# Routed expert loops: the turn and the split of the next tile's rows, one weight chunk sooner

## The chip, the core and the metric

The kernel is one program on one core of one Trainium2 chip. Its time is the device time of that core in microseconds (us), from one launch to its end; three runs give a median. Five engines work side by side, each with its own in-order queue: TensorE (PE in the profile, PEld for its weight loads), VectorE (DVE), ScalarE (ACT), GpSimd (POOL) and SyncE (SP, which issues most of the DMAs here). They meet through semaphores only.

## What is computed

Four layers of a gated cross-attention network on 16 sequences of 128 rows of 256 numbers. Each layer adds an attention part and a feed-forward part to x. The feed-forward parts of the first two layers are mixtures of eight experts, of which every row takes two; these are what the change touches. The second one, in the reference:

```python
logits = xt @ router_w.T + routing_bias
probs = jax.nn.sigmoid(logits)
topk_p, topk_idx = jax.lax.top_k(probs, TOP_K)          # TOP_K = 2 of E = 8
...
g = jnp.einsum('th,eih->tei', xt, wg)                    # I = 512
u = jnp.einsum('th,eih->tei', xt, wu)
h = jax.nn.silu(g) * u
y = jnp.einsum('tei,ehi->teh', h, wd)
routed = jnp.einsum('te,teh->th', w, y)
```

The first layer's is of the same form with 1024 in place of 512 and biases b1, b2 and b3; silu is on its first half too.

## The kernel before

**Tiles and chunks.** A router stage sorts the 2 x 2048 (row, expert) pairs by expert into 24 tiles, each of one expert: 15 big ones ("B") of 256 rows and 9 small ones ("S") of 128, in the fixed order BBSBBSBS, three times. `expert_tiles` then runs the same loop for both layers: as `l0m_e` (call in `l0_moe`, from about 297 to 668 us) with NF = 8 chunks of 128 hidden columns, and as `l1m_e` (call in `l1_moe`, from about 938 to 1143 us) with NF = 4. `count(t, f)` = NF t + f numbers the chunks.

**Two-part numbers.** Each fp32 operand is split into a high and a low part, and each product is three matmuls. For a chunk of up weights U, ACT makes the high part UH (line 1645) and DVE the low part UL = U - UH (1720). For the down weights DN, ACT makes DH (1655) and POOL makes DL (1812). For the hidden values ACT makes HH (1676, 1679) and DVE HL (1746, 1749). For the rows of a tile, which PE has turned into columns in PSUM (1561), ACT makes CH (1684) and DVE CL (1755). UH, UL, DH and DL are rings of four chunks; the columns, the weights and the rows have two buffers, by the tile's parity.

**One step (t, f)**, in the order of each queue:

- PE: `up(t, f)` (12 matmuls in a big tile, 6 in a small one; lines 1581, 1588, with a bias matmul at 1594 in l0m_e), `down(t - 1, f)` (6 or 3 matmuls, 1614), for small tiles the turning of their hidden values (1601), and in one step of the tile `turn(t + 1)`, four transposes or two. `up(t, 0)` waits for CH and CL of its tile, every `up` for its UH and UL, every `down` for its DH, DL, HH and HL.
- ACT: UH for the chunk two ahead, DH for two ahead of the down work, HH, silu (1664, 1667), then in one step CH of the next tile, `cols_high(t + 1)`. UH of a tile's first chunk waits for the landing of that tile's up weights. In l1m_e the copy of finished results (1690) stands in front at f = 1.
- DVE: UL for two ahead, the product with silu (1731, 1734, 1738), HL, and in one step CL, `cols_low(t + 1)`. In l0m_e the finished results (1763) stand here at f = 1.
- POOL: DL for each chunk of its tile, after f = 1 the gathers of tile t + 3 (1792, one DMA for each 128 rows), later in the tile the scatters of tile t - 1's results (1801).
- SP: the up weights of tile t when UL of tile t - 2 is done (1444), its down weights when DL of tile t - 2 is done (1455), one after the other.

PE runs down(t - 1) beside up(t), so POOL's DL of a tile is used one tile later than UL of the same tile. The order is written out by hand in the five queues; no planner moves anything. In both loops the step with the turn, CH and CL is f = NF // 2: after chunk 4 of 8, and after chunk 2 of 4.

Of the kernel before, what the change touches and what calls it, by code (L numbers as in the profile page):

```python
# [88 lines left out]
def build(nc, I, out):  # L89
# [20 lines left out]
    with top:  # L110
# [1355 lines left out]
        def expert_tiles(tag, weights, TAB, fill=None, place=None):  # L1466
# [4 lines left out]
            NF = FF // P  # L1471
# [3 lines left out]
            tiles = len(KIND)  # L1475
# [19 lines left out]
            with ExitStack() as c:  # L1495
# [31 lines left out]
                with nc.Block(no_gpsimd_drain=True) as block:  # L1527
# [26 lines left out]
                    def _(pe):  # L1554
# [43 lines left out]
                        def turn_hidden(u):  # L1598
                            pe.wait_ge(s_hr, u + 1)
                            for h in range(2):  # L1600
                                ins = nc.tensor.transpose(pair(hb(u))[:, h, 0:P], HR[:, u % 4, h * P:(h + 1) * P], IDENT)
                            ins.then_inc(s_ht, 1)

                        def down(t, f):
                            n = count(t, f)
                            pe.wait_ge(s_dh, n + 1)
                            pe.wait_ge(s_dl, n + 1)
                            pe.wait_ge(s_hh, at_unit[t, f] + 1)
                            pe.wait_ge(s_hl, at_unit[t, f] + 1)
                            if f == 0 and t >= 2:  # L1610
                                pe.wait_ge(s_ycopy, t - 1)
                            for r in range(R(t)):
                                for p, (h, w) in enumerate(((HH, DH), (HH, DL), (HL, DH))):
                                    ins = nc.tensor.matmul(yb(t)[:, r, :], h[:, t % 2, f, r * P:(r + 1) * P],  # L1614
                                                           w[:, f % RING, :],
                                                           start=(f == 0 and r == 0 and p == 0),
                                                           stop=(f == NF - 1 and r == R(t) - 1 and p == 2),
                                                           skip_group_check=True)
                            ins.then_inc(s_y, 1)
# [5 lines left out]
                        for t in range(tiles + 1):  # L1625
                            for f in range(NF):
                                if t < tiles:
                                    up(t, f)
                                if t >= 1:
                                    down(t - 1, f)  # L1630
                                for u in turn_at.get((t, f), ()):
                                    turn_hidden(u)
                                if f == NF // 2 and t + 1 < tiles:
                                    turn(t + 1)

                    @block.scalar
                    def _(act):
                        def up_high(n):
                            t, f = divmod(n, NF)
                            if t < tiles:  # L1640
                                if f == 0:
                                    act.wait_ge(s_up[t % 2], weights.up_count(t))
                                if n >= RING:
                                    act.wait_ge(s_up_done, n - RING + 1)
                                nc.scalar.copy(UH[:, f % RING, :, :, :],  # L1645
                                               U[:, t % 2, :, :, f * P:(f + 1) * P]).then_inc(s_uh, 1)

                        def down_high(n):
                            t, f = divmod(n, NF)
                            if 0 <= t < tiles:  # L1650
                                if f == 0:
                                    act.wait_ge(s_down[t % 2], 16 * (t // 2 + 1))
                                if n >= RING:
                                    act.wait_ge(s_y, n - RING + 1)
                                nc.scalar.copy(DH[:, f % RING, :], DN[:, t % 2, f, :]).then_inc(s_dh, 1)  # L1655

                        def silu(u):
                            t, f = units[u]
                            if u >= 4:
                                act.wait_ge(s_hr, u - 3)  # L1660
                            if big(t):
                                act.wait_ge(s_up_done, count(t, f) + 1)
                                kw = dict(bias=BU[:, t % 2, 0, f:f + 1]) if bias else {}
                                ins = nc.scalar.activation(SG[:, u % 4, :], hb(u)[:, 0:SLOTS], ACT.Silu, **kw)  # L1664
                            else:
                                act.wait_ge(s_up_done, count(t, f) + 2)
                                ins = nc.scalar.activation(pair(SG[:, u % 4, :]), pair(hb(u))[:, :, 0:P], ACT.Silu)
                            ins.then_inc(s_silu, 1)

                        def hidden_high(u):  # L1670
                            t, f = units[u]
                            if t >= 2:
                                act.wait_ge(s_y, count(t - 2, f) + (1 if big(t) else 2))
                            if big(t):
                                act.wait_ge(s_hr, u + 1)
                                ins = nc.scalar.copy(HH[:, t % 2, f, :], HR[:, u % 4, :])
                            else:
                                act.wait_ge(s_ht, turned(u))
                                ins = nc.scalar.copy(HH[:, t % 2, f:f + 2, 0:P], pair(hb(u))[:, :, 0:P])
                            ins.then_inc(s_hh, 1)  # L1680

                        def cols_high(t):
                            act.wait_ge(s_turn, t + 1)
                            nc.scalar.copy(CH[:, t % 2, :, 0:R(t) * P], cols_v(t)).then_inc(s_ch, 1)

                        def out_rows(t):
                            act.wait_ge(s_y, count(t + 1, 0))
                            if t >= 2:
                                act.wait_ge(s_store[t % 2], rows_upto(t - 2))
                            nc.scalar.copy(Y[:, t % 2, 0:R(t), :], yb(t)).then_inc(s_ycopy, 1)  # L1690

                        if fill is not None:
                            fill.act(act, *fill.EXPERTS)
                        up_high(0)
                        up_high(1)
                        cols_high(0)
                        for t in range(tiles + 1):
                            for f in range(NF):
                                if not bias and f == 1 and t >= 2:
                                    out_rows(t - 2)  # L1700
                                up_high(count(t, f) + 2)
                                down_high(count(t - 1, f) + 2)
                                for u in split_at.get((t, f), ()):
                                    hidden_high(u)
                                if t < tiles and ends(t, f):
                                    silu(at_unit[t, f])
                                if f == NF // 2 and t + 1 < tiles:
                                    cols_high(t + 1)
                        if not bias:
                            out_rows(LAST)  # L1710

                    @block.vector
                    def _(dve):
# [39 lines left out]
                        def cols_low(t):  # L1753
                            dve.wait_ge(s_ch, t + 1)
                            nc.vector.tensor_tensor(CL[:, t % 2, :, 0:R(t) * P], cols_v(t),  # L1755
                                                    CH[:, t % 2, :, 0:R(t) * P].bitcast(F32), ALU.subtract).then_inc(s_cl, 1)
# [14 lines left out]
                        for t in range(tiles + 1):  # L1771
                            for f in range(NF):
                                up_low(count(t, f) + 2)
                                if t < tiles and ends(t, f):
                                    hidden(at_unit[t, f])
                                for u in split_at.get((t, f), ()):
                                    hidden_low(u)
                                if bias and f == 1 and t >= 2:
                                    out_rows(t - 2)
                                if f == NF // 2 and t + 1 < tiles:  # L1780
                                    cols_low(t + 1)
                        if bias:
                            out_rows(LAST)
# [1976 lines left out]
```

## Time and profile before

| | us |
|---|---|
| runs | 1606.39, 1607.42, 1613.87 |
| median | 1607.42 |
| profiled execution, its own time | 1603.92 |
| its span, first to last instruction | 1602.1 |
| PE busy over the span | 1324.1 (83%) |
| DVE busy | 1130.4 (71%) |
| ACT busy | 906.0 (57%) |
| POOL busy | 728.4 (45%) |
| mean granted TensorE clock, of full speed | 0.912 |

A busy time is the sum of an engine's instruction times; a matmul's end is modelled, 0.28 us after its start where the next one starts 0.12 us after it. "Idle before, releaser" is the time an engine stood before an instruction and what ended it; "issue" means that the profile shows nothing it waited for. Start times are from the span's start.

### The profile page before, as it was taken

To read this page: it belongs to the slowest core of one execution; us is meant where nothing else is said; L and a number is where in the kernel's file an instruction comes from. 1 tells how busy PE (TensorE), PEld (TensorE's weight loads), DVE (VectorE), ACT (ScalarE), POOL (GpSimd) and SP (SyncE) were. 2 spreads that over 40 slices of the span, in tenths; PEclk is the share of its full clock that TensorE was granted. 3 is DMA by queue.
4 is the path that set the end of the run, shared out by engine and by line. 5 is a ranking of instruction groups with operands and counts; after the bars stand their busy time and mean duration, and the time that the engine had idled before them with its cause. 6 is when DMAs were issued, how large, how long until landed. Compare 5 with 4: busy or idle time off the path is not lost. (4 is left out here: it accounts for less than half of the span.)

```text
span 1602.1 us, 28284 instructions
## 1 busy us (share of the span) xinstructions
PE 1324.1 (83%) x9624; PEld 1110.0 (69%) x9642; DVE 1130.4 (71%) x2469; ACT 906.0 (57%) x1952; POOL 728.4 (45%) x753
## 2 busy tenths in 40 slices
PE   2689977899999999869974779899778965555898
PEld 0445555799999999735554779899776842345687
DVE  6447756688988988559966558778565649785654
ACT  3236652677877877457732447777426347464432
POOL 2223202367777777413321038888403930454444
PEclk8699997999999999889995789999899979676899
DMA  5000003456656656320014027676511000101000
GB/s 186 1 1 1 1 14 127 180 221 247 269 219 258 262 216 258 109 63 1 1 56 166 4 91 250 225 242 240 184 39 50 1 0 1 33 1 62 1 27 27
DMA packets 60780, 173.69 MB, mean 108 GB/s; under 512 B 10256, under 2 KB 42000, under 8 KB 51040
## 3 DMA queue, kind: packets, MB, share of 16 engines
q1 hardware_dynamic: 53152, 151.42, 26.4%
q0 software_dynamic: 7488, 20.46, 3.7%
q8 instruction: 81, 1.33, 0.4%
q14 instruction: 59, 0.48, 0.1%
HBM read 155.34 MB, written 16.52 MB: 107 GB/s over the span
## 5 line engine op out<-in xcount | busy, mean ns | idle before, releaser
L1812 POOL TENSOR_TENSOR l0m_e_DL<-l0m_e_DN,l0m_e_DH 128x256 fp32r<-128x256 f32 x192 | 183.4, 965 | 86.6 <-ACT l0m_e_DH L1655 85.5
L1720 DVE TENSOR_TENSOR l0m_e_UL<-l0m_e_U,l0m_e_UH 128x512 fp32r<-128x512 f32 x192 | 164.5, 862 | 10.7 <-ACT l0m_e_UH L1645 10.4
L1581 PE MATMUL PS<-l0m_e_CH,l0m_e_UH 128*128 128x256 f32 x480 | 138.5, 289 | 2.0 <-DVE l0m_e_CL L1755 2.0
L1581 PE MATMUL PS<-l0m_e_CH,l0m_e_UL 128*128 128x256 f32 x480 | 136.5, 284 | 0.0
L1581 PE MATMUL PS<-l0m_e_CL,l0m_e_UH 128*128 128x256 f32 x480 | 136.4, 284 | 0.0
L1645 ACT CAST l0m_e_UH<-l0m_e_U 128x512 fp32r<-128x512 f32 x192 | 118.1, 615 | 0.0
L1720 DVE TENSOR_TENSOR l1m_e_UL<-l1m_e_U,l1m_e_UH 128x512 fp32r<-128x512 f32 x96 | 85.5, 892 | 19.9 <-ACT l1m_e_UH L1645 19.2
L1812 POOL TENSOR_TENSOR l1m_e_DL<-l1m_e_DN,l1m_e_DH 128x256 fp32r<-128x256 f32 x96 | 85.2, 899 | 25.5 <-ACT l1m_e_DH L1655 24.4
L1581 PEld LDWEIGHTS PS<-l0m_e_CH,l0m_e_UH 128*128 128x128 f32 x480 | 92.8, 193 | 2.2 <-ACT l0m_e_UH L1645 2.2
L1581 PEld LDWEIGHTS PS<-l0m_e_CL,l0m_e_UH 128*128 128x128 f32 x480 | 92.9, 194 | 0.0
L1581 PEld LDWEIGHTS PS<-l0m_e_CH,l0m_e_UL 128*128 128x128 f32 x480 | 92.7, 193 | 0.0
L1614 PE MATMUL PS<-l0m_e_DH,l0m_e_HH 128*128 128x256 f32 x312 | 89.0, 285 | 4.1 <-issue 3.9
L1614 PE MATMUL PS<-l0m_e_DH,l0m_e_HL 128*128 128x256 f32 x312 | 88.6, 284 | 0.0
L1614 PE MATMUL PS<-l0m_e_DL,l0m_e_HH 128*128 128x256 f32 x312 | 88.6, 284 | 0.0
L1655 ACT CAST l0m_e_DH<-l0m_e_DN 128x256 fp32r<-128x256 f32 x192 | 78.1, 408 | 0.2 <-PE PS L1614 0.2
L1581 PE MATMUL PS<-l1m_e_CH,l1m_e_UH 128*128 128x256 f32 x240 | 71.8, 299 | 7.7 <-DVE l1m_e_CL L1755 6.2
L3505 POOL TENSOR_TENSOR Z<-l3f_WI,Z 128x512 f32<-128x512 f32 x32 | 50.7, 1586 | 58.6 <-DVE Z L3601 53.5
L1734 DVE SCALAR_TENSOR_TENSOR Z<-PS,l0m_e_BU,Z 128x256 f32<-128x256 f32 x120 | 57.4, 478 | 27.7 <-ACT Z L1664 27.3
L525 POOL TENSOR_TENSOR l1a_KBD<-CTX,CONST 128x512 f32<-128x512 f32 x32 | 33.1, 1039 | 92.7 <-PE PS L548 48.2
L525 POOL TENSOR_TENSOR l0a_KBD<-l0a_KT,CONST 128x512 f32<-128x512 f32 x32 | 33.4, 1046 | 91.3 <-PE PS L548 62.6
L1645 ACT CAST l1m_e_UH<-l1m_e_U 128x512 fp32r<-128x512 f32 x96 | 59.7, 623 | 24.6 <-DMA l1m_e_U<-in_l_up 18.5
L1746 DVE TENSOR_TENSOR l0m_e_HL<-Z,l0m_e_HH 128x256 fp32r<-128x256 f32 x120 | 72.5, 604 | 0.0
(610 smaller groups left out, 4752.9 us busy)
## 6 DMA issues: line engine op xcount, KB each, us to landing
l0m_e_U<-in_l_up SPq DMA_DIRECT2D x24, 2048.0 KB
l0m_e_DN<-in_l_down SPq DMA_DIRECT2D x24, 1024.0 KB, 5.0
l1m_e_U<-in_l_up SPq DMA_DIRECT2D x24, 1024.0 KB, 6.4
l1m_e_DN<-in_l_down SPq DMA_DIRECT2D x24, 512.0 KB, 3.9
CTX<-in_ctx SPq DMA_DIRECT2D x2, 2048.0 KB, 10.4
l1a_GA<-results_by_choice SPq DMA_DIRECT2D x16, 256.0 KB, 6.0
l1m_c_GA<-results_by_choice SPq DMA_DIRECT2D x16, 256.0 KB, 4.7
Z<-in_l_b_rows SPq DMA_DIRECT2D x24, 128.0 KB
```

What stands on the lines that cost most here:

```text
L525: nc.gpsimd.tensor_tensor(KBD[:, h % KR, :, :], KT[:, chunk, b * S:(b + 1) * S].rearrange("p (o s) -> p o s", o=1) .broadcast_to([P, 4, S] ...
L1581: ins = nc.tensor.matmul(hb(u)[:, a * SLOTS:(a + 1) * SLOTS], w[:, f % RING, k, a, :], x[:, t % 2, k, :], start=(p == 0), stop=(p == len(p ...
L1614: ins = nc.tensor.matmul(yb(t)[:, r, :], h[:, t % 2, f, r * P:(r + 1) * P], w[:, f % RING, :], start=(f == 0 and r == 0 and p == 0), stop= ...
L1645: nc.scalar.copy(UH[:, f % RING, :, :, :], U[:, t % 2, :, :, f * P:(f + 1) * P]).then_inc(s_uh, 1)
L1655: nc.scalar.copy(DH[:, f % RING, :], DN[:, t % 2, f, :]).then_inc(s_dh, 1)
L1720: nc.vector.tensor_tensor(UL[:, f % RING, :, :, :], U[:, t % 2, :, :, f * P:(f + 1) * P], UH[:, f % RING, :, :, :].bitcast(F32), ALU.subtr ...
L1734: ins = nc.vector.scalar_tensor_tensor(out=HR[:, u % 4, :], in0=hb(u)[:, SLOTS:2 * SLOTS], scalar=BU[:, t % 2, 1, f:f + 1], in1=SG[:, u % ...
L1746: ins = nc.vector.tensor_tensor(HL[:, t % 2, f, :], HR[:, u % 4, :], HH[:, t % 2, f, :].bitcast(F32), ALU.subtract)
L1812: nc.gpsimd.tensor_tensor(DL[:, f % RING, :], DN[:, t % 2, f, :], DH[:, f % RING, :].bitcast(F32), ALU.subtract).then_inc(s_dl, 1)
L3505: nc.gpsimd.tensor_tensor(HR(u), HA(u), HB(u), ALU.add).then_inc(s_h, 1)
```

## The change

In each of the three compute queues the step in which the next tile's rows are turned (PE), made into CH (ACT) and into CL (DVE) is one earlier: f = NF // 2 - 1, which is 3 instead of 4 in l0m_e and 1 instead of 2 in l1m_e. The place within the step stays the last. Nothing else is touched, no instruction is added or taken out, and each wait stays with its instruction.

```diff
@@ @block.tensor
                                 for u in turn_at.get((t, f), ()):
                                     turn_hidden(u)
-                                if f == NF // 2 and t + 1 < tiles:
+                                if f == NF // 2 - 1 and t + 1 < tiles:
                                     turn(t + 1)
@@ @block.scalar
                                 if t < tiles and ends(t, f):
                                     silu(at_unit[t, f])
-                                if f == NF // 2 and t + 1 < tiles:
+                                if f == NF // 2 - 1 and t + 1 < tiles:
                                     cols_high(t + 1)
@@ @block.vector
                                 if bias and f == 1 and t >= 2:
                                     out_rows(t - 2)
-                                if f == NF // 2 and t + 1 < tiles:
+                                if f == NF // 2 - 1 and t + 1 < tiles:
                                     cols_low(t + 1)
```

## Rows read from the trace of the kernel before

**Rows 1.** Windows, a stretch inside each loop: busy us (instructions), clock, DMA share, GB/s

```profile
core 0: us, PE busy (x) PEld busy (x) DVE busy (x) ACT busy (x) POOL busy (x), PEclk, DMA share, GB/s
320.00:650.00 330.00, 328.78 (x2758) 328.35 (x2758) 290.92 (x502) 260.39 (x655) 241.60 (x242) 1.00 0.63 240
960.00:1128.00 168.00, 157.64 (x1283) 153.64 (x1282) 135.37 (x230) 127.64 (x333) 141.69 (x146) 1.00 0.69 240
```

**Rows 2.** Waits, 320 to 650 us: who <- whom: total us, times, longest

```profile
DVE l0m_e_CL L1755 <- ACT l0m_e_CH L1684: 10.8, 8, 1.7
...
PE PS L1614 <- issue: 1.2, 2, 0.6
```

**Rows 3.** Waits, 900 to 1160 us, around L1's loop

```profile
ACT l1m_e_UH L1645 <- DMA l1m_e_U<-in_l_up: 18.5, 15, 2.5
...
ACT l1m_e_CH L1684 <- PE PS L1561: 13.5, 13, 4.8
...
PE PS L1581 <- DVE l1m_e_CL L1755: 6.2, 7, 1.5
...
PE PS L1561 <- DMA l1m_e_ROW<-rows_by_token,l1m_TOKEN: 5.6, 1, 5.6
...
PE PS L1588 <- DVE l1m_e_CL L1755: 2.3, 2, 1.6
...
PE PS L1581 <- issue: 1.5, 7, 0.3
```

**Rows 4.** Timeline, tile 8 to 9 of L1: start, us, engine, what, [idle before]

```profile
1012.47 0.62 ACT L1645 CAST l1m_e_UH<-l1m_e_U 128x512 fp32r<-128x512 f32 x1 [2.14 <-DMA l1m_e_U<-in_l_up]
...
1013.19 0.69 DVE L1720 TENSOR_TENSOR l1m_e_UL<-l1m_e_U,l1m_e_UH 128x512 fp32r<-128x512 f32 x1 [1.74 <-ACT l1m_e_UH L1645]
...
1013.81 0.28 PE L1614 MATMUL PS<-l1m_e_DH,l1m_e_HL 128*128 128x256 f32 x1
1013.88 0.58 ACT L1684 CAST l1m_e_CH<-PS 128x512 fp32r<-128x512 f32 x1
...
1014.35 0.63 ACT L1645 CAST l1m_e_UH<-l1m_e_U 128x512 fp32r<-128x512 f32 x1
...
1014.69 0.68 DVE L1755 TENSOR_TENSOR l1m_e_CL<-PS,l1m_e_CH 128x512 fp32r<-128x512 f32 x1
...
1015.63 0.36 PE L1581 MATMUL PS<-l1m_e_CH,l1m_e_UH 128*128 128x256 f32 x1 [1.54 <-DVE l1m_e_CL L1755]
```

**Rows 5.** Waits of POOL, 960 to 1128 us

```profile
POOL l1m_e_DL L1812 <- ACT l1m_e_DH L1655: 11.7, 17, 1.1
```

**Rows 6.** Timeline of POOL in L1's loop: three second DLs of a tile

```profile
981.36 0.74 POOL L1812 TENSOR_TENSOR l1m_e_DL<-l1m_e_DN,l1m_e_DH 128x256 fp32r<-128x256 f32 x1 [0.40 <-ACT l1m_e_DH L1655]
...
1015.36 1.22 POOL L1812 TENSOR_TENSOR l1m_e_DL<-l1m_e_DN,l1m_e_DH 128x256 fp32r<-128x256 f32 x1 [0.88 <-ACT l1m_e_DH L1655]
...
1116.20 0.94 POOL L1812 TENSOR_TENSOR l1m_e_DL<-l1m_e_DN,l1m_e_DH 128x256 fp32r<-128x256 f32 x1 [1.04 <-ACT l1m_e_DH L1655]
```

**Rows 7.** Timeline of PE in L1's loop: first tile, a down step, an "issue" boundary

```profile
940.56 0.55 PE L1581 MATMUL PS<-l1m_e_CH,l1m_e_UH 128*128 128x256 f32 x1 [1.49 <-DVE l1m_e_CL L1755]
...
1002.81 0.35 PE L1614 MATMUL PS<-l1m_e_DH,l1m_e_HH 128*128 128x256 f32 x1 [1.22 <-issue]
...
1006.02 0.35 PE L1581 MATMUL PS<-l1m_e_CH,l1m_e_UH 128*128 128x256 f32 x1 [0.17 <-issue]
```

**Rows 8.** Timeline of DVE and PE in L0's loop, tile 8, chunks 4 to 6

```profile
427.75 1.22 DVE L1720 TENSOR_TENSOR l0m_e_UL<-l0m_e_U,l0m_e_UH 128x512 fp32r<-128x512 f32 x1
...
429.79 0.68 DVE L1755 TENSOR_TENSOR l0m_e_CL<-PS,l0m_e_CH 128x512 fp32r<-128x512 f32 x1
...
430.13 0.28 PE L1581 MATMUL PS<-l0m_e_CH,l0m_e_UH 128*128 128x256 f32 x1
...
430.38 0.93 DVE L1720 TENSOR_TENSOR l0m_e_UL<-l0m_e_U,l0m_e_UH 128x512 fp32r<-128x512 f32 x1
```

**Rows 9.** The page's costliest groups: busy us, mean ns | idle before, releaser

```profile
L1812 POOL TENSOR_TENSOR l0m_e_DL<-l0m_e_DN,l0m_e_DH 128x256 fp32r<-128x256 f32 x192 | 183.4, 965 | 86.6 <-ACT l0m_e_DH L1655 85.5
...
L1812 POOL TENSOR_TENSOR l1m_e_DL<-l1m_e_DN,l1m_e_DH 128x256 fp32r<-128x256 f32 x96 | 85.2, 899 | 25.5 <-ACT l1m_e_DH L1655 24.4
```

## The prediction, made before the changed kernel had run

> **What bounds the kernel now.** The page makes TensorE (PE) the busiest engine, at 83% of the span, but a share is an average, so I asked for stretches. The diff touches only the two routed loops, L0's (8 weight chunks a tile) and L1's (4 chunks a tile). In L0's loop PE is busy for 328.78 of 330 us, at a granted clock of 1.00, which is the 2.4 GHz level; in L1's it is 157.64 of 168, at the same clock [rows 1]. So the change can win only in L1, about 10 us at most, and can lose in L0. The waits say what the gaps are. In L0 PE waited 1.2 us in all, never for the split columns CL [rows 2]. In L1 it waited for CL 6.2 + 2.3 us in nine places, and seven waits of 1.5 us in all stand as "issue" [rows 3]. Those seven are of the same kind: each is the first up matmul of a tile, as at 1006.02 [rows 7], and starts about 0.25 us after a CL ended, as the labelled ones do.
>
> One boundary shows the mechanism [rows 4]. PE turns tile 9's rows in chunk 2 of tile 8, but ScalarE (ACT) sits until 1012.47 for the landing of tile 9's up weights, then has DH, HH and a silu in its queue, so CH starts at 1013.88, VectorE (DVE) makes CL from 1014.69 to 1015.37, and PE, whose last matmul issued at 1013.81 (they issue 0.12 apart), goes on at 1015.63. UL of the new tile had been ready at 1013.88.
>
> The other engine to look at is GpSimd (POOL), which makes DL and issues the gathers and scatters. From 960 to 1128 us it is busy 141.69 us and waits 11.7 us, on 17 occasions, for DH [rows 1, 5]; most of the remaining 14.6 us are the gaps around its DMA instructions, 0.15 to 0.3 each. With those it is (168 - 11.7) / 168 = 93% full: PE's slack and POOL's are the same size.
>
> **The change, part by part.** Steps (t, f) are tile t, chunk f. The turn, CH and CL of tile t+1 go from step NF/2 to NF/2 - 1: from 4 to 3 in L0, 2 to 1 in L1, for 23 tiles in each loop. No instruction is added or removed.
>
> PE: the four (or two) transposes cost the same in either place: 0. They now need the gathered rows one step earlier, 18 matmuls of 0.12 or 2.2 us in a big tile. Only one turn of L1's loop ever waited for rows, the first, 5.6 us with the issue of its gathers in it [rows 3]; POOL issues the gather of tile t+3 after the second DL of tile t, which is a tile and more before its turn, 5.8 us at the least. The landing has to be slower than in that first case for anything to show: 0, and up to 2.2 us a tile if that cover were gone. POOL's gather waits on the turn's semaphore, which now comes earlier: nothing there. SP is moved past nothing: its loads wait for UL(t,3) and DL, which stand ahead of CH and CL in their queues both before and after.
>
> What goes at the L1 boundaries: start-to-start idle less the 0.12 issue step. The nine labelled waits and seven "issue" ones sum to 10.0; one of them, 1.49, is the loop's first tile, whose columns are made before the loop and don't move [rows 3, 7]: 8.5 left at 15 boundaries. The profile counts idle from a matmul's modelled end, 0.28 after its start, and the next could issue after 0.12, so each gives 0.16 more: 8.5 + 15 x 0.16 = **10.9 us** on PE. What is late next at those boundaries is UL(t+1,0): at 1013.88 it was ready 0.05 before PE was (1013.81 + 0.12) [rows 4], so that gap shrinks from 1.70 to about 0.2; at the other boundaries UL was further ahead.
>
> Does it arrive at the end? Only if POOL follows, since every down step takes a DL. PE already stands for POOL in small tiles, whose steps are 12 matmuls or 1.44 us and where two gathers sit between two DLs: 1.22 before 1002.81 is the longest [rows 7]. POOL's own waits are for DH, and eleven of the seventeen, the first 0.40 before 981.36 and the last 1.04 before 1116.20 [rows 6], are before the second DL of a tile, whose DH stands in ACT's queue right behind CH and one UH. They sum to 8.0. With CH gone from there ACT comes to that DH 0.47 sooner (1013.88 to 1014.35 [rows 4]) where CH ran at once, and by CH's wait for the turn as well where it had one (13.5 us over 13 tiles, 4.8 of them in the first [rows 3]). Two of the eleven (0.88 before 1015.36 is one [rows 6]) follow a weight landing that nothing here hastens: they give 0.47 each of 0.88. 8.0 - 2 x 0.41 = **7.2 us**. The six others stand behind landings or PE's pace: I leave them. PE's 10.9 can't outrun this by more than the 1 to 3 us by which DL is ready ahead of use, and it loses that lead at the next small tile. The weight loads are issued when a DL is done, so they come forward with POOL and no further. The smaller side carries: 7.2.
>
> What CH costs in its new place: it now stands ahead of UH(t+1,0) and DH(t,0), and ACT waits for the turn there. Bounds: 0 where the landing is late anyway (15 tiles, 18.5 us of wait [rows 3]), and 0.47 plus a wait for the turn otherwise, a wait that has been 8.7 / 12 = 0.7 us (13.5 less the first 4.8). POOL comes to DH(t,0) late, from its scatters, so most of this is covered; I take 0 and keep half of it for the 8 other tiles, 8 x 0.6 = 5 us, for the range.
>
> L0: DVE now makes CL after chunk 3, ahead of UL(t,6). In tile 8, UL(8,6) ran 427.75 to 428.97 and PE took it at 430.13: 1.16 to spare; CL takes 0.59 of DVE's queue (429.79 to 430.38) [rows 8]. That leaves 0.57, and about 0.25 is what PE needs after an end (1015.37 to 1015.63 [rows 4]). UL(t,7), which no longer stands behind CL, gains. I take 0, bounds -0.5 and +5. There is nothing to gain, PE having no wait for CL.
>
> Sum: 0 + 0 + 0 - 7.2 = -7.2 us. The profiled execution took 1603.92 (span 1602.1 and 1.8 around it): it would be 1596.7. The median of the three runs is 3.5 above it, 1607.42, which gives **1600.2**.
>
> The Trainium skill, page "SBUF — State Buffer", section "SBUF: two separate sides", says that a VectorE operation with both inputs in SBUF and a GpSimd one that reads SBUF exclude each other for a whole instruction. The trace agrees in kind: one DL took 1.22 us [rows 6] where the mean is 0.899 [rows 9]. By that rule a denser loop stretches DL; this is the second rival.
>
> **Rivals.** (1) PE's gaps close in full, POOL giving way too: its 11.7 us of waits allow it. 1607.4 - 10.9 = 1596.5. Against it: POOL's landings. (2) POOL becomes the bound by itself: DL and UL meet more often. L0's loop, with DVE busy for 88% against 81% [rows 1], shows a mean DL of 965 ns against 899 in L1 [rows 9]. At L0's mean, 96 x 0.066 = 6.3 us come back: gain 0.9, 1606.5. (3) Slower: DVE in L0. CL stands at chunk 3 waiting for CH, with UL(t,6) queued behind it and PE behind that. From 1.0 us of delay on, PE waits; at 1.5 us, 23 x 0.5 = 11.5 us lost against 7.2 won: 1611.7. For it: DVE waited for CH 8 times, up to 1.7 us [rows 2]. Against: a DVE that waits has nothing late behind it, and the spare computed above. (4) No effect: something else, a late weight landing, ends each wait at the same time: 1607.4.
>
> **How the numbers follow.** Forecast (gain 4 to 9) 0.60, (1) 0.12, (2) 0.18, (3) 0.06, (4) 0.04. Range: from the full gain and a microsecond of scatter, 1595.5, to just past (2), 1607.0; outside lie (3), (4) and a tail. About 0.5% (8 us) is what a measurement of this kernel can tell from no change: more than 8.0 of gain takes all of (1) and a third of the forecast, 0.33; slower by as much takes the worse part of (3), 0.05; the rest 0.62.
>
> **What would show it.** In the changed profile: no PE wait for CL in L1 after the first tile (7.0 + 1.5 us gone); CH starting right after the turn; ACT's waits for up weights as long or longer (18.5); POOL's waits for DH down from 11.7 to about 4 in the same tiles; PE's waits on L1614 in small tiles grown by 2 to 4 us; the L1 loop, 940.6 to about 1140, 7 us shorter; L0's PE still within 2 us of full. Wrong, if PE in L0 shows waits for UL (L1720), if L1's boundaries wait for UL or UH instead, or if mean DL is near 0.965.

## The result, and the profile after

The changed kernel took 1596.68 us in the median of 16 runs (1592.06 to 1607.20), the kernel before 1604.12 in the median of 16 (1598.60 to 1613.87): 7.4 us or 0.46% less by the medians. The ratio estimated from these runs is 0.9946, 95% interval 0.9930 to 0.9962: a gain of 0.54%, between 0.38% and 0.70%, or 6 to 11 us. No change lies far outside that interval; the 0.5% that the prediction took as its line lies inside it. The profiled execution took 1595.48 us, 8.4 less than that of before (1603.92).

**Where the time went.** Three views of the changed kernel answer the first rows of before. The windows, with the columns of rows 1:

```profile
320.00:650.00 330.00, 328.34 (x2757) 328.00 (x2756) 294.06 (x503) 262.55 (x655) 232.06 (x242) 1.00 0.64 240
960.00:1128.00 168.00, 161.35 (x1332) 158.97 (x1331) 141.11 (x240) 133.35 (x346) 146.53 (x151) 1.00 0.71 245
```

In L0's loop PE stays full (328.34 us against 328.78). In the same 168 us of L1's loop it now gets through 1332 matmuls where it had 1283, POOL through 151 instructions where it had 146.

The waits of the changed kernel, PE and ACT from 900 to 1160 us, and POOL from 960 to 1128 us (who <- whom: total us, times, longest), answer rows 3 and 5:

```profile
PE PS L1614 <- DVE l1m_e_HL L1749: 2.8, 5, 0.8
...
PE PS L1614 <- issue: 2.4, 4, 0.8
...
PE PS L1581 <- DVE l1m_e_CL L1755: 1.5, 1, 1.5
...
PE PS L1614 <- ACT l1m_e_DH L1655: 1.1, 1, 1.1
...
PE PS L1614 <- ACT l1m_e_place L1690: 0.8, 1, 0.8
PE PS L1581 <- ACT l1m_e_UH L1645: 0.7, 1, 0.7
PE PS L1588 <- issue: 0.2, 1, 0.2
```

```profile
ACT l1m_e_CH L1684 <- PE PS L1561: 13.0, 18, 4.8
...
ACT l1m_e_UH L1645 <- DMA l1m_e_U<-in_l_up: 5.9, 5, 1.9
```

```profile
POOL l1m_e_DL L1812 <- ACT l1m_e_DH L1655: 6.4, 13, 1.3
```

PE's waits for CL are gone, all but the one of the first tile, and so are the seven "issue" ones at L1581. Two short waits stand at up matmuls in their place, 0.7 us for UH and 0.2 us of "issue". The rest is on L1614, the down matmuls.

The length of the loop is read from the first and the last matmul of two groups (least/median/most ns, first to last start). This is the changed kernel:

```profile
L1581 PE MATMUL PS<-l1m_e_CH,l1m_e_UH x240: 277/283/553, 941.2 to 1124.3; 128*128 128x256 f32 x120
...
L1614 PE MATMUL PS<-l1m_e_DL,l1m_e_HH x156: 278/283/283, 950.9 to 1135.2; 128*128 128x256 f32 x156
```

and this the kernel before:

```profile
L1581 PE MATMUL PS<-l1m_e_CH,l1m_e_UH x240: 278/283/550, 940.6 to 1130.6; 128*128 128x256 f32 x120
...
L1614 PE MATMUL PS<-l1m_e_DL,l1m_e_HH x156: 274/283/283, 950.8 to 1141.6; 128*128 128x256 f32 x156
```

From 940.6 to 1141.6 are 201.0 us; from 941.2 to 1135.2 are 194.0. L0's loop, measured likewise, took 368.3 us in both. So 7.0 of the 8.4 us of span lie in L1's loop. The rest is scatter: what follows the loop took 460.5 us in this execution of the kernel before and 458.5 in that of the changed one, but 457.4 and 456.6 in two more executions of unchanged L1 code (runs 1 and 3).

**The boundary of tile 8 to 9**, ACT in the changed kernel (start, us, engine, what, [idle before]), which answers rows 4:

```profile
1011.35 0.59 ACT L1684 CAST l1m_e_CH<-PS 128x512 fp32r<-128x512 f32 x1 [0.35 <-PE PS L1561]
1011.98 0.62 ACT L1645 CAST l1m_e_UH<-l1m_e_U 128x512 fp32r<-128x512 f32 x1
1012.50 0.40 ACT L1655 CAST l1m_e_DH<-l1m_e_DN 128x256 fp32r<-128x256 f32 x1
```

CH runs as soon as the turn is there, ahead of the first UH of tile 9. The 2.14 us in which ACT stood for that tile's weights are gone: it stands 0.35 for the turn and finds the weights landed.

### The profile page after: what moved, and what is told of

Read it like the earlier page. It is cut to its first block and busy times, and to the rows that moved or that the text cites. A ratio compares the mean times of both kernels' runs of the same rounds, so it can differ in the third digit from the quotient of the medians.

```text
span 1593.7 us, 28302 instructions
## 1 busy us (share of the span) xinstructions
PE 1323.9 (83%) x9642; PEld 1110.3 (70%) x9642; DVE 1131.5 (71%) x2469; ACT 909.3 (57%) x1952; POOL 719.7 (45%) x753
## 5 line engine op out<-in xcount | busy, mean ns | idle before, releaser
L1812 POOL TENSOR_TENSOR l0m_e_DL<-l0m_e_DN,l0m_e_DH 128x256 fp32r<-128x256 f32 x192 | 175.2, 922 | 96.6 <-ACT l0m_e_DH L1655 95.2
L1720 DVE TENSOR_TENSOR l0m_e_UL<-l0m_e_U,l0m_e_UH 128x512 fp32r<-128x512 f32 x192 | 168.7, 884 | 10.9 <-ACT l0m_e_UH L1645 10.4
L1581 PE MATMUL PS<-l0m_e_CH,l0m_e_UH 128*128 128x256 f32 x480 | 138.4, 288 | 2.0 <-DVE l0m_e_CL L1755 2.0
L1581 PE MATMUL PS<-l0m_e_CL,l0m_e_UH 128*128 128x256 f32 x480 | 136.5, 284 | 0.0
L1581 PE MATMUL PS<-l0m_e_CH,l0m_e_UL 128*128 128x256 f32 x480 | 136.5, 284 | 0.0
L1812 POOL TENSOR_TENSOR l1m_e_DL<-l1m_e_DN,l1m_e_DH 128x256 fp32r<-128x256 f32 x96 | 86.9, 921 | 16.6 <-ACT l1m_e_DH L1655 15.5
L1581 PEld LDWEIGHTS PS<-l0m_e_CH,l0m_e_UH 128*128 128x128 f32 x480 | 92.7, 193 | 2.2 <-ACT l0m_e_UH L1645 2.2
L1581 PEld LDWEIGHTS PS<-l0m_e_CH,l0m_e_UL 128*128 128x128 f32 x480 | 92.8, 193 | 0.0
L1581 PEld LDWEIGHTS PS<-l0m_e_CL,l0m_e_UH 128*128 128x128 f32 x480 | 92.8, 193 | 0.0
L1614 PE MATMUL PS<-l0m_e_DH,l0m_e_HH 128*128 128x256 f32 x312 | 89.0, 285 | 4.5 <-issue 2.6
L1720 DVE TENSOR_TENSOR l1m_e_UL<-l1m_e_U,l1m_e_UH 128x512 fp32r<-128x512 f32 x96 | 83.1, 868 | 11.2 <-ACT l1m_e_UH L1645 10.7
L1614 PE MATMUL PS<-l0m_e_DH,l0m_e_HL 128*128 128x256 f32 x312 | 88.6, 284 | 0.0
L1614 PE MATMUL PS<-l0m_e_DL,l0m_e_HH 128*128 128x256 f32 x312 | 88.5, 284 | 0.0
L1734 DVE SCALAR_TENSOR_TENSOR Z<-PS,l0m_e_BU,Z 128x256 f32<-128x256 f32 x120 | 57.3, 478 | 24.2 <-ACT Z L1664 23.8
L1581 PE MATMUL PS<-l1m_e_CH,l1m_e_UH 128*128 128x256 f32 x240 | 70.9, 295 | 2.2 <-DVE l1m_e_CL L1755 1.5
L1664 ACT ACTIVATE Z<-PS,l0m_e_BU 128x256 f32<-128x256 f32 x120 | 56.9, 474 | 23.1 <-PE PS L1581 21.0
```

What stands on the lines that cost most here:

```text
L1581: ins = nc.tensor.matmul(hb(u)[:, a * SLOTS:(a + 1) * SLOTS], w[:, f % RING, k, a, :], x[:, t % 2, k, :], start=(p == 0), stop=(p == len(p ...
L1720: nc.vector.tensor_tensor(UL[:, f % RING, :, :, :], U[:, t % 2, :, :, f * P:(f + 1) * P], UH[:, f % RING, :, :, :].bitcast(F32), ALU.subtr ...
L1734: ins = nc.vector.scalar_tensor_tensor(out=HR[:, u % 4, :], in0=hb(u)[:, SLOTS:2 * SLOTS], scalar=BU[:, t % 2, 1, f:f + 1], in1=SG[:, u % ...
L1812: nc.gpsimd.tensor_tensor(DL[:, f % RING, :], DN[:, t % 2, f, :], DH[:, f % RING, :].bitcast(F32), ALU.subtract).then_inc(s_dl, 1)
```

## The experiments

All lengths of L1's loop below are measured as above. In the kernel before it was 201.0 us, in two more executions of unchanged L1 code 202.0 and 202.0: 201.7 in the mean. With the change it was 194.0, 193.6 and 194.5: 194.0 in the mean. **The change is worth 7.6 us in this loop**, and executions repeat the length within 1 us, while whole times of one kernel scatter by 15 us over 16 runs and by 25 over 33. Runs 5, 8, 9, 10 and 12 were each one execution. Expectations that name 199.1 and 361.5 us for the loops of before, and 192 for L1's after, count to an earlier down group of the last tile; the same executions give 201.0, 368.3 and 194.0 here.

**1. The kernel before once more.** No edit.

> The kernel before, unchanged, against itself: how far two sets of runs of one kernel lie apart, and how long its two routed loops and the stages after them take in a second profiled execution. Every theory: ratio 1.000 within 0.002; L0's loop (first up matmul to the last down group) 361.5 us, L1's 199.1 us, as in the first profile. If what follows L1's loop (462.4 us in the first profile, 460.3 in the changed kernel's) varies by 2 us here too, that part of the measured 8.4 us of span is scatter between executions and not the change; if it comes out at 462.4 again, the change reaches it.

Measured: 1605.38 us against 1606.05, ratio 0.9995 (0.9969 to 1.002), loops 368.3 and 202.0. What follows L1's loop took 457.4 us, against 460.5 in the first profile: it varies by 3 us without any change, so that part of the 8.4 us is scatter, as the first branch of the expectation has it.

**2. The change in L1 alone**, in all three places:

```diff
-if f == NF // 2 and t + 1 < tiles:
+if f == NF // 2 - (1 if bias is None else 0) and t + 1 < tiles:
```

> The change in L1's loop alone (4 chunks a tile), L0's loop as before. Theory: all of the gain is here: L1's loop 192 us, 7.0 us less than before, ratio 0.9946 to 0.996. Rival, that L0's loop or the wider re-timing gives part: a gain clearly under that of the whole change, with L1's loop above 193.

Measured: 1596.51 us, ratio 0.9947 (0.9926 to 0.9967), loops 368.3 and 193.6.

**3. The change in L0 alone:**

```diff
-if f == NF // 2 and t + 1 < tiles:
+if f == NF // 2 - (0 if bias is None else 1) and t + 1 < tiles:
```

> The change in L0's loop alone (8 chunks a tile), L1's loop as before. Theory: nothing, ratio 1.000 within 0.002, L0's loop 361.5 us as before, because TensorE is full there and never waited for the split columns. Rival: a gain of 1 to 2 us from vector-engine order, or a loss because the columns' low part now stands ahead of the low part of the weights of chunk 6.

Measured: 1608.05 us, ratio 1.0016 (0.9989 to 1.0043), loops 368.3 and 202.0. The whole effect is L1's, and L0's part is nothing either way.

**4. The whole change once more:**

> The changed kernel again, beside the two halves on the same chip. Theory: 7.0 us from L1's loop (192.2 us), and what the stages after it add is scatter, so the ratio over five rounds lies near 0.9955, between 0.9946 and 0.9962. Rival: the stages behind L1's loop gain 1 to 2 us of their own, the ratio stays at 0.9946 or under and the profile again has 460.3 us or less behind the loop.

Measured: 1596.68 us against 1606.05, ratio 0.996 (0.9938 to 0.9983), L1's loop 194.5. The expected 0.9946 to 0.9962 came.

**5. One chunk later than before**, L1 at chunk 3 of 4 (`NF // 2 + (1 if bias is None else 0)`):

> The other way: in L1's loop the turn, CH and CL one chunk later than before (chunk 3, the last of the tile), L0 as before. L1's loop, first up matmul to last down matmul, was 201.0, 202.0 and 202.0 us in three profiles of the kernel before. Theory, that the wait at a tile's first up matmul is for the split columns and hangs on their place: PE now waits at each of 23 boundaries for turn, CH and CL one after the other, 0.3 + 0.6 + 0.7 us and the hops between them at the least, 2 to 3.5 us each: 45 to 80 us of waits for CL in place of 7, loop 235 to 270. Rival, that something else ends nearly every wait (weights or POOL): loop under 212.

Measured: 1634.32 us (before 1606.12), L1's loop 233.1, just below the 235 expected: 31 us lost. Waits of PE in this kernel, 938 to 1176 us:

```profile
PE PS L1581 <- DVE l1m_e_CL L1755: 26.5, 15, 2.1
...
PE PS L1588 <- DVE l1m_e_CL L1755: 6.1, 3, 2.0
```

The wait that the change removed grows to 32.6 us in 18 places, less than the 45 to 80 of the expectation. That is 24.1 more than before, the largest part of the 31 us. Not all of it is this wait: PE also stood 6.8 us for UH, and its busy time for the same 1518 matmuls was 5.5 us longer (195.2 us from 938 to 1180, against 189.7 from 938 to 1145 before), at a granted clock of 0.95 against 0.98.

**6. Two chunks sooner than before**, `NF // 2 - 2` in all three places:

> Turn, CH and CL two chunks sooner than before in both loops (chunk 2 of 8, chunk 0 of 4). Theory, that one chunk removed every wait for CL and the rest of the loop is set by POOL's queue, by landings and by the hidden values of small tiles: no further gain, L1's loop 193 to 196 us against 194.0 for one chunk. Rival, that still earlier columns keep paying because they leave ACT's and DVE's queues alone near the boundary: 190 to 192.

Measured: 1610.73 us, ratio 1.002 (0.9992 to 1.0049), L1's loop 205.4 (L0's 369.2). My theory had 193 to 196; it missed by more than 9 us. PE did not wait for CL, yet the loop was longer than before the change. Its waits, and ACT's and POOL's, 900 to 1160 us:

```profile
ACT l1m_e_CH L1684 <- PE PS L1561: 20.9, 19, 4.8
...
POOL l1m_e_DL L1812 <- ACT l1m_e_DH L1655: 23.1, 19, 7.1
...
PE PS L1614 <- DVE l1m_e_HL L1749: 4.8, 10, 0.9
```

CH at chunk 0 stands in ACT's queue ahead of the fourth UH of tile t and the fourth DH of tile t - 1, while PE comes to the turn only after the up and down matmuls of the step. Which DL this makes late is counted under run 10.

**7. The turn alone one chunk further ahead** than in the change (PE at `NF // 2 - 2`, CH and CL at `NF // 2 - 1`), so that ACT finds it done:

> As the changed kernel, but TensorE turns the rows one chunk before CH is due (chunk 0 of 4, chunk 2 of 8), CH and CL stay at chunk 1 and 3. ACT then no longer stands for the turn (13.0 us over 18 waits in the changed kernel, 4.8 of them in the first tile). Theory, that ACT's queue with this wait in it makes DH and UH late behind CH: 1 to 3 us more gain, L1's loop 191 to 193. Rival, that ACT has that slack and POOL or the weights set the pace: 194 as with the change, within 1 us.

Measured: 1601.02 us, ratio 0.9965 (0.9933 to 0.9996), L1's loop 196.1 (L0's 369.5), neither the 191 to 193 of the theory nor, by a microsecond, the rival's 193 to 195. ACT's waits for the turn were gone after the first, and it waited 13.7 us on 12 occasions for up weights instead.

**8 and 9. No gathers in L1's loop**, in the kernel before and in the changed one, so that POOL has two DMA instructions less in a big tile and one in a small one, 34 in all:

```diff
-if f == 1 and t + 3 < tiles:
+if bias and f == 1 and t + 3 < tiles:
     gather(t + 3)
```

> The kernel before with the gathers of tiles 3 to 23 left out of L1's loop (each tile reads rows that are already there), 34 gather instructions of 1.0 us and gaps of 0.15 to 0.3, some 43 us of POOL's queue. Its partner with the change on top follows. Theory, that POOL holds back only what comes after the boundary waits are gone: the waits for CL stay at 8 us or grow, the loop shrinks by 2 to 5 us, to 197 to 200. Rival, that POOL was the bound before the change too: 190 to 194.

> The changed kernel with the gathers of tiles 3 to 23 left out of L1's loop, the partner of the run that left them out of the kernel before (L1's loop there 196.6 us against 201.7 with gathers: 5.1 less, POOL waiting 59.0 us for DH). With gathers the change is worth 7.6 us of this loop. Theory, that POOL's queue takes back a part of TensorE's 10.9: without it the change is worth 8.5 to 11, loop 185.6 to 188. Rival, that the part not won goes elsewhere (hidden values of small tiles, landings, ACT standing for the turn): the change is worth 7 to 8 here too or less, loop 188.5 or more.

Measured: L1's loop 196.6 without the change (just under what was expected; the waits for CL, expected at 8 us or more, fell from 8.5 to 5.4) and 187.6 with it, so the change is worth 9.0 us without gathers, against 7.6. Whole times: 1595.36 and 1597.1 us, the second at a lower mean granted clock (0.907 against 0.913); its stretches ahead of L0's loop and behind L1's were 5 to 6 us longer. That POOL had room shows in its waits in the first of the two, 900 to 1160 us; under them PE's there (lines stand one higher in these two kernels):

```profile
POOL l1m_e_DL L1813 <- ACT l1m_e_DH L1656: 59.0, 66, 6.8
```

```profile
PE PS L1582 <- DVE l1m_e_CL L1756: 5.0, 6, 1.5
...
PE PS L1615 <- DVE l1m_e_HL L1750: 3.3, 4, 0.9
...
PE PS L1582 <- issue: 1.4, 8, 0.2
...
PE PS L1589 <- DVE l1m_e_CL L1756: 0.4, 1, 0.4
```

Counted as in the prediction, these are 5.0 + 1.4 + 0.4 less the first tile's 1.5, and 14 x 0.16: 7.5 us at the boundaries. All of that is gone with the change, and PE's wait for HL fell from 3.3 to 2.1 as well; a new wait of 0.3 stands at the turning of a small tile's hidden values. That is 8.4 us in all, against 9.0 measured. **Without gathers the change gives back all that PE lost at the boundaries; with them it gives 7.6 of 10.9.** This is the prediction's main step, and it rests on one execution of each of the two kernels without gathers. It doesn't separate POOL's room from VectorE's: without gathers the 96 ULs of the loop kept VectorE busy for 72.3 us before the change and 76.1 with it, against 84.2 to 85.5 and 76.2 to 83.1 with gathers.

**10. CH at chunk 0 with CL at chunk 1**, in L1 only: which of the two does the harm in run 6?

```diff
-if f == NF // 2 and t + 1 < tiles:            # PE and ACT
+if f == (0 if bias is None else NF // 2) and t + 1 < tiles:
-if f == NF // 2 and t + 1 < tiles:            # DVE
+if f == (1 if bias is None else NF // 2) and t + 1 < tiles:
```

> L1's loop only: turn and CH at chunk 0, CL at chunk 1; L0 as before. With all three at chunk 0 the loop took 205.4 us, with the turn alone at chunk 0 196.1, with all at chunk 1 194.0. Theory, that CH at chunk 0 is what costs, because ACT stands for the turn (20.9 us over 19 waits) with UH, DH and the silu of its next steps behind it: 202 to 206. Rival, that CL is: VectorE standing for CH ahead of UL at chunk 0: 194 to 198.

Measured: 1602.02 us, L1's loop 203.2, as the theory had it. CL is not needed for the harm, and the turn alone at chunk 0 gave 196.1 (run 7): it is CH. Two lines of its waits, 900 to 1160 us (the second was 19.2 before and 10.7 with the change):

```profile
ACT l1m_e_CH L1684 <- PE PS L1561: 22.0, 18, 4.8
...
DVE l1m_e_UL L1720 <- ACT l1m_e_UH L1645: 30.0, 21, 2.7
```

The four DLs of a tile show what stands behind CH. This is POOL's wait for DH in the whole of L1's loop by the DL before which it stood, us (times), without the first DL of all:

| CH, at the end of chunk | 1st DL | 2nd | 3rd | 4th | DH right behind CH |
|---|---|---|---|---|---|
| 2 (before) | 1.0 (2) | 11.8 (14) | 0.8 (2) | 4.2 (5) | the 2nd |
| 1 (the change) | 2.1 (2) | 3.2 (8) | 0.3 (1) | 2.7 (6) | the 1st |
| 0 (run 6) | 0.6 (2) | 2.0 (4) | 0.7 (1) | 12.7 (11) | the 4th, of the tile before |
| 0 (run 10) | 0.6 (1) | 2.9 (5) | 0.3 (1) | 16.0 (14) | the same |

POOL comes to the first DL from the scatters and to the third from the gathers, and hardly waits there in any of the four. It comes to the second and the fourth from another DL. The change moves the late DH from the second DL to the first, where the scatters cover it; one chunk more moves it to the fourth, where nothing does.

**11. The changed kernel with the turn between a step's up and down matmuls**, not behind both, so that CH finds it done without being moved:

```diff
 if t < tiles:
     up(t, f)
+if f == NF // 2 - 1 and t + 1 < tiles:
+    turn(t + 1)
 if t >= 1:
     down(t - 1, f)
 ...
-if f == NF // 2 - 1 and t + 1 < tiles:
-    turn(t + 1)
```

> As the changed kernel, but within the step TensorE turns the rows before its down matmuls instead of after them, so that ACT has the columns 0.7 us sooner (in a big tile) and the rows are needed hardly any sooner. ACT stood 13.0 us over 18 waits for the turn with the change. Theory, that this standing costs what is left between 7.6 and 10.9: 1 to 3 us more gain, L1's loop 191 to 193. Rival, as the turn a whole chunk ahead showed (196.1), ACT's earlier start only meets later landings and fuller POOL and VectorE queues: 193.5 to 196.5.

Measured: 1597.43 us against 1605.91, ratio 0.9926 (0.9901 to 0.9951), L1's loop 193.6. The ratio's interval overlaps that of the change, and the loop is as long as the changed kernel's (193.6 to 194.5), so I don't call it faster than the change: the rival's 193.5 to 196.5 came. ACT's waits, 900 to 1160 us:

```profile
ACT l1m_e_UH L1645 <- DMA l1m_e_U<-in_l_up: 14.8, 14, 2.5
...
ACT l1m_e_CH L1684 <- PE PS L1561: 4.8, 1, 4.8
```

The waits for the turn, 8.2 us after the first in the changed kernel, are gone, and 8.9 more stand at the weights' landing (14.8 against 5.9). ACT waits as long as before in another place, and nothing comes of it at the end.

**12. The changed kernel without the weight loads of tiles 2 to 23 in L1:** are the landings the next bound?

```diff
-if t >= 2:                                    # SP, up weights and down weights
+if bias and t >= 2:
-act.wait_ge(s_up[t % 2], weights.up_count(t))
+act.wait_ge(s_up[t % 2], weights.up_count(t if bias else t % 2))
...                                            # the same for DVE
-act.wait_ge(s_down[t % 2], 16 * (t // 2 + 1))
+act.wait_ge(s_down[t % 2], 16 * (t // 2 + 1) if bias else 16)
```

> The changed kernel with the expert weights of tiles 2 to 23 not loaded in L1's loop (each tile uses the weights of tile 0 or 1 that are already there). What is left of TensorE's 10.9 us after the change's 7.6 is some 3.3; without gathers 1.4 of it came back. If landings hold the rest: loop 191 to 192.5 against 194.0, ACT's 5.9 us of waits for up weights gone and with them TensorE's waits for UH. Rival, that landings are covered once the columns are sooner, and the rest is small tiles' hidden values and DL queued on POOL: 193 to 195.

Measured: 1599.9 us, L1's loop 193.4. My theory had 191 to 192.5, the rival 193 to 195. With every landing out of the way the loop gained 0.6 us, which is within its scatter. So in the changed kernel the landings are covered, and the waits for them only fill ACT's spare time. PE's longest waits in the loop were still on the down matmuls, 938 to 1160 us:

```profile
PE PS L1614 <- issue: 4.0, 7, 1.4
```

**Together**, the place of turn, CH and CL in L1's four chunks against the length of its loop:

| chunk | 3 | 2 (before) | 1 (the change) | 0 |
|---|---|---|---|---|
| L1's loop, us | 233.1 | 201.7 | 194.0 | 205.4 |

The two in the middle are means of three executions, the outer ones single executions.

## Why the prediction was right or wrong

**Right: the place.** All of it is in L1 (run 2: 0.9947; run 3: 1.0016), L0 gives nothing. The spare that the prediction worked out for L0 went as it said. In the changed kernel, tile 8 of L0 (DVE):

```profile
428.04 0.68 DVE L1755 TENSOR_TENSOR l0m_e_CL<-PS,l0m_e_CH 128x512 fp32r<-128x512 f32 x1
428.64 1.32 DVE L1720 TENSOR_TENSOR l0m_e_UL<-l0m_e_U,l0m_e_UH 128x512 fp32r<-128x512 f32 x1
```

UL(8,6) ends at 429.96 and PE takes it at 430.42: 0.46 to spare where there were 1.16, and 0.57 had been forecast. In tiles 6 and 22 it is 0.23, about what PE needs after an end, and no wait for UL arose. Rival 3 (slower through L0's DVE) needed 1.0 us of delay, and there were 0.7. Instead DVE's waits for CH in L0's loop fell from 10.8 us to 4.3, both times in eight places.

**Right: PE's side, nearly in full.** The gaps in front of the up matmuls of the loop, start to start less 0.12 and without the first tile's, sum to 10.9 us before and to 1.2 after: 0.8 for UH at one boundary and 0.3 of "issue". So 9.7 of the 10.9 closed. The forecast had allowed for UL as the next in line, with 0.2 at one boundary.

**Right: POOL's waits before its second DL go, and less arrives than PE gave up.** Forecast: 7.2 at the end of 10.9. Measured: 7.6 in the loop, 7.4 in the medians; and 9.0, about all that there was, without gathers. From 960 to 1128 us the waits before second DLs fell from 8.0 us (11 times) to 2.4 (6 times), 5.6 where the forecast had 7.2, and the others stayed, from 3.7 us to 4.0, as it had left them. The page's group of DL in the whole of L1 (busy us, mean ns | idle before):

```profile
L1812 POOL TENSOR_TENSOR l1m_e_DL<-l1m_e_DN,l1m_e_DH 128x256 fp32r<-128x256 f32 x96 | 86.9, 921 | 16.6 <-ACT l1m_e_DH L1655 15.5
```

Its wait for DH fell from 24.4 us [rows 9] to 15.5, by 8.9, and its busy time grew by 1.7. That is 7.2 us. The agreement with the forecast to the tenth is luck: the same two numbers in run 1's execution of the unchanged kernel were 21.7 and 87.8 (mean 925). Nor is this sum a proof of its own, since the rest of POOL's work stays and waits and DLs together must shrink about as the loop does.

**Refuted: rivals 1, 2 and 4.** Rival 1 (the full 10.9) named 1596.5, which is the time that came, but by its mechanism the loop would have been 190.8 long, and it was 194.0. Rival 2 wanted a mean DL of 965; it is 921 after and 899 and 925 in two executions of the unchanged kernel. Rival 4 fell with runs 2 and 5.

**Wrong: what a measurement can tell, and through it the likeliest outcome.** The step that failed is "About 0.5% (8 us) is what a measurement of this kernel can tell from no change". No row stood behind it. The interval of the measured ratio is 0.16% (2.6 us) to either side, so the forecast's own 7.2 us, 0.45%, would have been told from no change, and the measured gain was. I gave 0.62 to a change that can't be told from none and 0.33 to faster, and the kernel is faster, by 0.54% by the ratio. Even with the line at 8 us an even split would have said what the sum knew: the forecast lay 0.8 us from it, and the interval of the measurement (0.38% to 0.70%) does not decide on which side the gain is.

**Mis-sized: the base.** I subtracted 7.2 from the median of three runs, 1607.42, and got 1600.2; over 16 runs the same kernel's median is 1604.12. The term is "the median of the three runs is 3.5 above it": it measured 0.2 above the profiled 1603.92. The profiled execution less 7.2 is 1596.7, the measured 1596.68; that the two agree so closely is luck, with runs from 1592.06 to 1607.20. The range (1595.5 to 1607.0) covered it.

**Mis-sized: POOL's own waits.** "Down from 11.7 to about 4 in the same tiles": they fell to 6.4 on 13 occasions (960 to 1128 us). The gain was not smaller for it: in the whole loop the fall was 8.9, and over three executions of each kernel it was 7.3 in the mean (24.4, 21.7 and 24.2 before; 15.5, 17.0 and 16.0 after).

**Wrong: ACT's landings.** I forecast its waits for up weights "as long or longer (18.5)" and they fell to 5.9 in five places. I had seen that CH would now stand ahead of UH(t+1,0), and had not followed it to the end: ACT spends time at the turn (13.0 us on 18 occasions, 13.5 on 13 before), and finds the weights landed. In run 11 the two traded almost one for one (8.2 us against 8.9). For the same reason "two of the eleven follow a weight landing that nothing here hastens" was beside the point; without any landings the changed kernel's loop is 0.6 shorter.

**Bounded, and it held: what CH costs in its new place.** I took 0 with a bound of 5. At chunk 1 it is 0 within what can be seen: run 7 and run 11 both free ACT from the wait for the turn, and gain nothing (196.1 and 193.6). At chunk 0 the same cost is about 9 to 11 us (203.2 and 205.4 against 194.0). The prediction's reason, "POOL comes to DH(t,0) late, from its scatters", is what the table under run 10 shows: 1.1 us more of wait before the first DLs with the change, and 10 to 13 more before the fourth ones at chunk 0.

**What took the rest of the 10.9.** In the kernel before, PE's waits on the down matmuls of L1 were these (938 to 1160 us):

```profile
PE PS L1614 <- issue: 1.7, 3, 1.2
...
PE PS L1614 <- ACT l1m_e_place L1690: 0.8, 1, 0.8
...
PE PS L1614 <- ACT l1m_e_DH L1655: 0.7, 2, 0.5
PE PS L1614 <- DVE l1m_e_HL L1749: 0.7, 1, 0.7
```

With 0.16 more for each, they grew from 5.0 to 8.9 us; 2 to 4 more had been forecast. (Closed 9.7 less grown 3.9 leaves 5.8 of this pair's 7.0; the rest stands in no listed gap.) I had put them down to POOL alone, but part is DVE's: HL of a small tile came late in five places, 2.8 us. This part varies: 2.9 in run 2, but 1.2 in run 4, against 0.7 to 1.2 in three executions of unchanged L1 code. In the changed kernel, tile 7 to 8 (DVE, then POOL, then PE):

```profile
1004.28 3.03 DVE L1720 TENSOR_TENSOR l1m_e_UL<-l1m_e_U,l1m_e_UH 128x512 fp32r<-128x512 f32 x2 [0.90 <-ACT l1m_e_UH L1645]
1007.23 0.41 DVE L1731 TENSOR_TENSOR l1m_e_place<-PS,l1m_e_place 128x256 f32<-128x256 f32 x1
1007.57 0.41 DVE L1749 TENSOR_TENSOR l1m_e_HL<-PS,l1m_e_HH 128x256 fp32r<-128x256 f32 x1
```

```profile
1004.28 1.00 POOL L1801 DMA_INDIRECT results_by_choice<-l1m_e_place,l1m_CHOICE  x1 [0.17 <-issue]
1005.31 1.44 POOL L1812 TENSOR_TENSOR l1m_e_DL<-l1m_e_DN,l1m_e_DH 128x256 fp32r<-128x256 f32 x2
```

```profile
1008.27 0.36 PE L1614 MATMUL PS<-l1m_e_DH,l1m_e_HH 128*128 128x256 f32 x1 [0.70 <-DVE l1m_e_HL L1749]
```

Two ULs took 3.03 us, where the median of one is 0.69. The first took 0.72; the second, from 1005.04, took 2.27, while POOL made two DLs; HL stood behind them, and PE behind HL. No run isolates this reading; the shorter ULs without gathers (runs 8 and 9) go with it. How the 3.3 us between 10.9 and 7.6 divide between the 1.2 left at the boundaries, POOL, HL and DH stays open. Runs 8 and 9 show only that the sum depends on the gathers. That a VectorE operation with both inputs in SBUF and a GpSimd operation that reads SBUF exclude each other is what the Trainium skill says (page "SBUF — State Buffer", section "SBUF: two separate sides"). By that rule the stretched one may be either; the prediction looked for the effect in DL only. Here it is UL. The trace agrees only in kind: it draws UL's start ahead of both DLs, so it does not show which of them held the other up.

## What to carry to other kernels

Where several engines work off queues in a fixed order, making a tile's inputs earlier has a best place; in this loop it was one of four. Earlier takes away a wait at the next tile's start, and puts the new work ahead of something else in its queue. So write down what will stand right behind it, who takes that next, and whether the taker is then busy with other work anyway. When the busiest engine's gaps are closed, look at the other engine that serves every step and count its gaps around DMA instructions as load; here a part of the gain did not arrive while that engine was 93% full. A wait that only fills spare time moves to another releaser when it is removed; before pricing one, ask who is late if it goes. And before naming a change too small to tell, work out the interval that the planned number of runs will give.

## What the runs showed of the hardware

One kernel's whole time scatters by more than this change is worth, and little of that scatter lies in L0's loop: it takes 367.8 to 369.5 us in all fourteen traces, of different kernels, and 368.3 in eight of them. Its granted clock is 0.99 over the loop in each, where the stretch behind L1's loop had 0.86 in the profiles before and after. Over the changed kernel's 16 runs the span goes with the mean granted clock: the four shortest (1590.2 to 1591.3 us) had 0.913 to 0.916, the ten between (1592.7 to 1599.5) 0.910 to 0.913, the two longest (1603.2 and 1605.3) 0.907 and 0.906. So an effect of half a per cent inside a loop was read from the loop's own length in a trace to within 1 us, where the whole times of 16 runs a side gave it to within 2.6.

A VectorE operation whose median is 0.69 us was seen to take up to 2.32 us in L1's loop of the changed kernel, and up to 2.47 in that of the kernel before. In the kernel's own group it is the longest of 96:

```profile
L1720 DVE TENSOR_TENSOR l1m_e_UL<-l1m_e_U,l1m_e_UH x96: 673/692/2317, 934.5 to 1129.0; 128x512 fp32r<-128x512 f32 x96
```

Waits labelled "issue" can be waits for data: of the seven at L1581 in L1, each 0.3 us at most [rows 3], none was left in the changed kernel's profile when CL came earlier, just as with the labelled ones. Executions differ in this: one such wait stood at L1581 again in run 2 (0.8 us) and in run 4 (0.4).
